# A tower of embedding, attention and routed experts on one core: VectorE's small operations dealt out among its products, and the order of TensorE's ups around the down

## The reference, cut to what matters

```python
z = jnp.einsum('nd,sdr->nsr', layernorm(h), P)
scores = jnp.einsum('nsr,smr->nsm', z, C)
topv, topi = jax.lax.top_k(scores, K)
w = jax.nn.softmax(topv, axis=-1)
hid = jax.nn.gelu(jnp.einsum('nsr,nskrh->nskh', z, W1[sidx, topi]) + b1[sidx, topi])
yl = jnp.einsum('nskh,nskhr->nskr', hid, W2[sidx, topi]) + b2[sidx, topi]
comb = jnp.einsum('nskr,nsk->nsr', yl, w).reshape(N, S * R)
out = h + jax.nn.gelu(comb @ G1 + g1b) @ G2 + g2b
```

## Time and profile before

| what | value |
| --- | --- |
| median of 3 runs | 2905.35 us |
| lowest and highest | 2901.58 and 2911.56 us |
| profiled execution, its own time | 2918.95 us |
| its span | 2917.2 us |
| TensorE matmul busy | 2477.4 us (85%) |
| VectorE busy | 1895.8 us (65%) |
| ScalarE busy | 1200.4 us (41%) |
| GpSimd busy | 1155.5 us (40%) |
| mean granted TensorE clock | 0.926 |

### The profile page before, as it was taken

How to read it: one execution, slowest core, us unless ns; L and a number is a source line. 1 busy time by engine, 2 the same in 40 slices (tenths; PEclk the granted TensorE clock), 3 DMA queues, 4 the chain that set the end, 5 groups by cost and what they waited for, 6 DMA issues and landing times. The chain is left out here.

```text
span 2917.2 us, 42124 instructions
## 1 busy us (share of the span) xinstructions
PE 2477.4 (85%) x16000; PEld 1240.8 (43%) x16000; DVE 1895.8 (65%) x3858; ACT 1200.4 (41%) x1617; POOL 1155.5 (40%) x781
## 2 busy tenths in 40 slices
PE   3556999999999999999999996048888888888898
PEld 1223555565555556555555653022323323232232
DVE  5865565565655656565555654147878888788786
ACT  3421333333333333333333332035656666566565
POOL 5000475666757566575756654021120111201010
PEclk9788999999999999999999998558989999798899
DMA  1002000000010000000000002810101011010100
GB/s 45 11 22 55 7 1 9 1 9 9 1 30 1 9 1 9 9 1 9 1 2 1 3 1 10 72 36 1 24 1 24 1 24 24 1 24 1 24 6 6
DMA packets 78699, 38.51 MB, mean 13 GB/s; under 512 B 62937, under 2 KB 71193, under 8 KB 77849
## 3 DMA queue, kind: packets, MB, share of 16 engines
q1 hardware_dynamic: 76320, 30.98, 6.2%
q10 hardware_dynamic: 640, 1.69, 0.5%
q0 software_dynamic: 1536, 3.15, 0.4%
HBM read 21.93 MB, written 10.49 MB: 11 GB/s over the span
## 5 line engine op out<-in xcount | busy, mean ns | idle before, releaser
L588 POOL TENSOR_TENSOR acc<-acc,pT 128x1024 f32<-128x1024 f32 (+3 forms) x412 | 830.0, 2015 | 243.7 <-ACT pT L907 210.4
L1615 DVE TENSOR_TENSOR hw<-hid,banks 128x512 f32<-128x512 f32 x1024 | 645.7, 683 | 192.0 <-PE banks L1358 187.3
L907 ACT ACTIVATE pT<-banks 128x1024 f32<-128x1024 f32 x480 | 405.7, 896 | 831.1 <-PE banks L661 818.2
L787 DVE TENSOR_REDUCE part<-banks 128x2 f32<-128x1024 f32 (+3 forms) x432 | 438.3, 1044 | 311.7 <-PE banks L637 310.0
L1487 ACT ACTIVATE hid<-banks 128x1024 f32<-128x1024 f32 x512 | 499.5, 1022 | 333.3 <-PE banks L1348 314.7
L1348 PE MATMUL banks<-zst,w1c 50*128 50x512 f32 x1024 | 425.9, 582 | 29.2 <-ACT hid L1487 23.3
L1358 PE MATMUL banks<-wT,select 64*128 64x512 f16 x1024 | 357.5, 421 | 61.6 <-DVE hw L1615 56.9
L677 PE MATMUL banks<-pT,v 128*64 128x512 f32 (+3 forms) x1920 | 404.7, 542 | 1.5 <-POOL pT L576 1.5
L1366 PE MATMUL banks<-hw,w 128*32 128x512 f32 x2048 | 302.0, 664 | 1.4 <-DVE hw L1615 0.8
L1358 PEld LDWEIGHTS banks<-wT,select 64*128 64x128 f16 x1024 | 98.9, 98 | 439.9 <-DVE hw L1615 355.7
L637 PE MATMUL banks<-kh,qh 64*128 64x512 f32 (+1 forms) x960 | 191.1, 393 | 14.5 <-ACT pT L907 5.6
(11 more groups left out here) (183 smaller groups left out, 2901.0 us busy)
## 6 DMA issues: line engine op xcount, KB each, us to landing
zst<-z_scratch SPq DMA_DIRECT2D x48, 128.0 KB, 4.4
z_scratch<-zp SPq DMA_DIRECT2D x8, 512.0 KB, 3.5
out_h<-o SPq DMA_DIRECT2D x8, 384.0 KB, 2.7
xT_scratch<-xs_hi SPq DMA_DIRECT2D x4, 512.0 KB, 2.7
xt_hi<-xT_scratch SPq DMA_DIRECT2D x2, 1024.0 KB, 5.6
w1c<-raw1p ACTq DMA_DIRECT2D x12, 132.0 KB, 4.6
w1c<-raw1p SPq DMA_DIRECT2D x12, 132.0 KB, 4.1
wo<-in_L_attn_W_O SPq DMA_DIRECT2D x12, 96.0 KB, 1.9
```

The source lines that it names most:

```text
L588: pool.tensor_tensor(acc[:, G % 2, :, off:CH], acc[:, G % 2, :, off:CH], pT[:, slot, :, 0:w], ALU.add).then_inc(summed, 1)
L787: last = dve.tensor_reduce(to[:, :, c:c + 1], both[:, :, 0:whole], AX.X, ALU.max)
L907: act.activation(pT[:, J % PSLOTS, :, 0:CH - off], both[:, :, 0:CH - off], ACT.Exp, scale=E ** -0.5)\
L1615: dve.tensor_tensor(hw[:, n % 2, q, :], hid[:, n % 2, q, :], ring_bank(("w", g, n, q)), ALU.mult).then_inc(mixed, 1)
```

## The change

The diff, without the lines of whole functions that only change their arguments (mix now makes one block and not two; normalise and the main loops go through pairs (n, q) and not steps n):

```diff
-        Z_AT = {16: (0,), 17: (1,), 20: (2,)}
-        PREP_AT = {12: (3, 4), 14: (5, 6), 26: (7,), 27: (8,), 28: (9,), 29: (10,)}
+        Z_AT = {11: (0,), 12: (1,), 13: (2,)}
+        PREP_AT = {5: (3, 4), 7: (5, 6), 24: (7,), 25: (8,), 27: (9,), 28: (10,)}
         OUT_AT = {1: (0,), 2: (1,), 3: (2,)}
-        EXP_AT = 18
-        SPLIT_AT = 22
-        BIAS_AT = (18, 21)
+        EXP_AT = 17
+        BIAS_AT = (18, 22)
+        BEST_FROM, MARK_FROM = 8, 16
+        KEEP_AT = {(20, 2): 0, (21, 2): 1, (24, 0): 2, (24, 2): 3}
+        HIGH_AT = {(23, 1): 0, (26, 1): 1}
+        DEN_AT, RECIPROCALS_AT = (16, 0), (20, 0)
+        SUMS_AT, VARIANCE_AT, REFINE_AT, SPLIT_AT = (5, 0), (7, 0), (9, 0), (15, 3)
+        TAKE_OUT_AT = {(3, 1): 0, (4, 1): 1}
...
             def divide(g, part):
-                pool.wait_ge(marked, 2 * g + part + 1)
+                pool.wait_ge(marked, 4 * g + 2 * part + 2)
...
-            def up(g, n, pair, which):
+            def up(g, n, pair, which, beside=None):
                 if which == 0:
                     need(pe, gelu_done, g * (2 * NSTEP) + 2 * n - 1 + pair)
-                low_rows = work(n)[2 * pair][1] < NJ // 2
-                i = 2 * pair + (which + 1 if low_rows else which) % 2
+                    first_of[pair] = 2 * pair
+                    if beside is not None:
+                        gw, nw, iw = beside
+                        first_of[pair] += work(nw)[iw][1] < NJ // 2
+                i = first_of[pair] if which == 0 else 4 * pair + 1 - first_of[pair]
...
                     spread_weights(g, n, 2)
                     if next1[0] < NG:
-                        up(*next1, 1, 0)
+                        up(*next1, 0, 1)
                     if g or n:
                         down(*last1)
                     spread_weights(g, n, 3)
                     if next1[0] < NG:
-                        up(*next1, 1, 1)
+                        up(*next1, 1, 0, (g, n, 3))
                         if next1[1] == 0:
                             pe.wait_ge(w_copied, next1[0] * 4 + 4)
                         spread_weights(*next1, 0)
-                    if next2[0] < NG:
-                        up(*next2, 0, 0)
-                    if next1[0] < NG:
+                        up(*next1, 1, 1)
                         spread_weights(*next1, 1)
                     if next2[0] < NG:
-                        up(*next2, 0, 1)
+                        up(*next2, 0, 0, (*next1, 1))
...
-            def top_four(g, k):
+            def best(g, m):
+                k, r = divmod(m, GT * S // 4)
                 t2, half = divmod(k, 2)
-                dve.wait_ge(side_free, freed_at["prep", g, 3 + k])
-                dve.memset(holder[:, k:k + 1], 0.0)
-                for t in (2 * t2, 2 * t2 + 1):
-                    for q in range(NQ):
-                        i = (half * NQ + q) * GT + t
-                        last = dve.max(top[:, i, :], sc[:, i, :])
-                if k == 3:
+                if r == 0:
+                    dve.wait_ge(side_free, freed_at["prep", g, 3 + k])
+                    dve.memset(holder[:, k:k + 1], 0.0)
+                i = (half * NQ + r % NQ) * GT + 2 * t2 + r // NQ
+                last = dve.max(top[:, i, :], sc[:, i, :])
+                if m == GT * S - 1:
                     link(last)
...
-            def mark(g, part):
-                for i in range(part * GT * S // 4, (part + 1) * GT * S // 4):
-                    last = dve.match_replace(scr[:, i, :], top[:, i, :], sc[:, i, :], TAKEN)
-                if part == 3:
+            def mark(g, i):
+                last = dve.match_replace(scr[:, i, :], top[:, i, :], sc[:, i, :], TAKEN)
+                if i % (GT * S // 4) == GT * S // 4 - 1:
                     link(last)
...
             def keep_marked(g, part):
-                half = slice(part * GT * S // 2, (part + 1) * GT * S // 2)
-                dve.scalar_tensor_tensor(ew[:, half, :], scr[:, half, 0:M], TAKEN, ew[:, half, :],
+                quarter = slice(part * GT * S // 4, (part + 1) * GT * S // 4)
+                dve.scalar_tensor_tensor(ew[:, quarter, :], scr[:, quarter, 0:M], TAKEN, ew[:, quarter, :],
                                          ALU.is_equal, ALU.mult).then_inc(marked, 1)
...
+            def choose(g, n, q):
+                if BEST_FROM <= n < BEST_FROM + 8:
+                    best(g, (n - BEST_FROM) * NQ + q)
+                if (n, q) == DEN_AT:
+                    denominators(g)
+                if MARK_FROM <= n < MARK_FROM + 8:
+                    mark(g, (n - MARK_FROM) * NQ + q)
+                if (n, q) == RECIPROCALS_AT:
+                    reciprocals(g)
+                if (n, q) in KEEP_AT:
+                    keep_marked(g, KEEP_AT[n, q])
+                if (n, q) in HIGH_AT:
+                    high_weights(g, HIGH_AT[n, q])
...
             for g in range(NG):
-                for n in range(NSTEP):
-                    mix(g, n, (0, 1))
-                    if g and n in (3, 4):
-                        take_out(g - 1, n - 3)
+                for n, q in GAPS:
+                    mix(g, n, q)
+                    if g and (n, q) in TAKE_OUT_AT:
+                        take_out(g - 1, TAKE_OUT_AT[n, q])
                     if g < NG - 2:
-                        normalise(g + 2, n)
-                    mix(g, n, (2, 3))
+                        normalise(g + 2, n, q)
                     if g < NG - 1:
-                        prepare(g + 1, n)
-                    if n == SPLIT_AT and g < NG - 2:
-                        split_z(g + 2)
+                        choose(g + 1, n, q)
```

More of the change, by code:

```diff
@@ L1410, in _ @@
             pe.wait_ge(w_copied, 4)
+            first_of = [0, 0]
             for n, pair in ((0, 0), (0, 1), (1, 0)):
                 up(0, n, pair, 0)
-                up(0, n, pair, 1)
+                if (n, pair) != (1, 0):
+                    up(0, n, pair, 1)
             for i in (0, 1):
@@ L1607, in high_weights, with mix @@
                 dve.tensor_copy(wsp[:, half, :, 0, :], by_half).then_inc(w_cast, 1)
-            def mix(g, n, blocks):
-                if (g or n > 1) and 0 in blocks:
+            def mix(g, n, q):
+                if (g or n > 1) and q == 0:
                     dve.wait_ge(down_done, g * NSTEP + n - 1)
-                for q in blocks:
-                    dve.wait_ge(gelu_done, g * (2 * NSTEP) + 2 * n + q // 2 + 1)
-                    dve.wait_ge(spread, g * (NQ * NSTEP) + NQ * n + q + 1)
-                    dve.tensor_tensor(hw[:, n % 2, q, :], hid[:, n % 2, q, :], ring_bank(("w", g, n, q)),
-                                      ALU.mult).then_inc(mixed, 1)
+                dve.wait_ge(gelu_done, g * (2 * NSTEP) + 2 * n + q // 2 + 1)
+                dve.wait_ge(spread, g * (NQ * NSTEP) + NQ * n + q + 1)
+                dve.tensor_tensor(hw[:, n % 2, q, :], hid[:, n % 2, q, :], ring_bank(("w", g, n, q)),
+                                  ALU.mult).then_inc(mixed, 1)
             def take_out(g, k):
@@ L1624, in take_out @@
                                   g2b_bc[:, :].unsqueeze(1).to_broadcast([P, 2, D]), ALU.add).then_inc(out_taken, 1)
-            def prepare(g, n):
-                if 14 <= n < 18:
-                    top_four(g, n - 14)
-                if n == 17:
+            def choose(g, n, q):
+                if BEST_FROM <= n < BEST_FROM + 8:
+                    best(g, (n - BEST_FROM) * NQ + q)
+                if (n, q) == DEN_AT:
                     denominators(g)
-                if 18 <= n < 22:
-                    mark(g, n - 18)
-                if n == 22:
+                if MARK_FROM <= n < MARK_FROM + 8:
+                    mark(g, (n - MARK_FROM) * NQ + q)
+                if (n, q) == RECIPROCALS_AT:
@@ L1634, in prepare, with normalise @@
                     reciprocals(g)
-                if n in (22, 23):
-                    keep_marked(g, n - 22)
-                if n in (24, 25):
-                    high_weights(g, n - 24)
-            def normalise(g, n):
-                if n == 7:
+                if (n, q) in KEEP_AT:
+                    keep_marked(g, KEEP_AT[n, q])
+                if (n, q) in HIGH_AT:
+                    high_weights(g, HIGH_AT[n, q])
+            def normalise(g, n, q):
+                if (n, q) == SUMS_AT:
@@ L1643, in normalise @@
                     sums(g)
-                if n == 13:
+                if (n, q) == VARIANCE_AT:
                     variance(g)
-                if n == 15:
+                if (n, q) == REFINE_AT:
                     refine(g)
+                if (n, q) == SPLIT_AT:
+                    split_z(g)
+            GAPS = [(n, q) for n in range(NSTEP) for q in range(NQ)]
             for g in range(2):
-                for n in range(NSTEP):
-                    normalise(g, n)
-                split_z(g)
@@ L1653, in _ @@
-            for n in range(NSTEP):
-                prepare(0, n)
+                for n, q in GAPS:
```

(11 more changed lines are left out.)

## The result

The changed kernel takes 2965.23 us (median of 4 runs, 2962.24 to 2966.89) against 2906.17 us for the kernel before: ratio 1.0201, 95% interval 1.0182 to 1.0221. It is 59 us slower. The forecast was 2941 us with a range of 2885 to 2985, and slower at 0.72. The profiled execution took 2965.44 us, span 2963.7 us, where the sum made against the profiled execution of before gave 2955.

A forecast was written before the change was run, and what follows sets the result against it. A chain through gelu, up and down set the 3.1 us step; after the change TensorE binds at 2.70 us. Steps, side work and waits sum to 986 us against 950.6, so 2955 profiled and 2941 us forecast, range 2885 to 2985.

The forecast's parts named there:

- The order of the ups: Experts' stage: no up waiting for the newest gelu precedes the down; clean step 3.1 to 2.70 us, 86.4 us a group.
- the circle that the prediction priced second: Clean step by way of VectorE: last product, hand-over, spreading and up, down, spreading to the next product, 2.68 us.
- Singly dealt: VectorE's largest findings and marks between products cost 0.14 and 0.20 us each; what exceeds 2.70 adds 7.9 us a group.
- The scores' wait: Scores moved from step 12 to 5: TensorE waits 9.0 us for z rows in groups 1 to 6; bounds 6 and 12.
- The weights' wait: Weights turned from step 24, not 26: TensorE waits 3.5 us for GpSimd's low half in seven groups; bounds 2 and 5.
- Banks held longer: Spreadings wait for ScalarE's later side copies; per group 0.5 us after mixture, 2.0 scores, 1.9 x and z, 3.6 weights.
- The sum: Experts' stage: groups of 118, five of 130.5, 125 and 90.3 us, together 986 us against 950.6, 36 us more.
- From the profiled execution to the median: Whole kernel: profiled execution to come to 2955 us, less 13.6 us it stood above the median, giving 2941 us.
- Half clock: Rival: granted clock falls to 1.2 GHz behind a gap, 3.4 us in each of seven groups; 2965 us, chance 0.18.
- The surpluses meet: Rival: VectorE's surplus in steps 16 to 24 is paid during TensorE's waits, 76 us less; 2865 us, chance 0.17.
- No change: Rival: half of the overlap of VectorE's surplus with TensorE's waits, 38 us; 2903 us, chance 0.08.
- serial pairs: Rival: spreading and up run one after the other, a step takes 3.5 us; over 3050 us, chance 0.07.

The follow-up runs named there:

- e7: The kernel before with the new order of the ups alone, tables and VectorE's batches of eight kept: 2899.40 us, 0.9964 of the kernel before.
- e4: Changed kernel with z bounce ahead of the output, GpSimd's first low half ahead of the second divide, ScalarE's copies ahead of the gelu: 2852.48 us, 0.9808 of the kernel before.
- e8: The kernel before with VectorE's largest findings and marks alone dealt out, two behind each product in the same steps: 2891.10 us, 0.9924 of the kernel before.
- e1: Changed kernel with SyncE's loop alone altered, z rows of group g + 2 bounced ahead of the output of group g: 2914.13 us, 1.0013 of the kernel before.
- e3: Changed kernel with ScalarE's copies of side items ahead of the first gelu of the step after next: 2945.04 us, 1.0127 of the kernel before.
- e5: Changed kernel with 38 float16 matmuls on 64 rows put on TensorE ahead of the z wait: 2995.37 us, 1.0292 of the kernel before.
- e10: Changed kernel with 38 matmuls on all 128 rows put on TensorE ahead of the z wait: 2961.15 us, 1.0173 of the kernel before.
- e2: Changed kernel with GpSimd's first low half of the weights ahead of the second divide: 2932.51 us, 1.0081 of the kernel before.

## Why the prediction was right or wrong

**The order of the ups.** Right in size: 2.66 us a clean step (2.70 forecast), last group 90.1 us (90.3). The bound is another than the text says. It has TensorE full, 4 x 0.43 + 1.0, but the three pairs behind the down take 0.96 us together and TensorE stands 0.28 us in the step for VectorE. What sets it is the circle that the prediction priced second, at 2.68: last product, spreading and up, down, spreading, next product. The two prices lay so near each other that the number doesn't tell them apart; the rows do. Side work adds to the step all the same: in e7 steps without it gain 0.4 us and those with it nothing, and in e4 a turned weight adds 0.6 us (3.3 against 2.7). Why the 0.28 us don't cover part of that was not tested. The sign that the gelus would no longer come in back-to-back pairs didn't show.

**Singly dealt.** Right in the price, 0.73 us for a product with its largest finding. The 7.9 us of this term can't be added up from the items as the text lists them, which come to about 11; some 7.9 is left if steps 11 to 13, 17, 18, 22 and 24 aren't counted, where another item is longer, and the text doesn't say so. Step 10, which has largest findings and nothing else, took the 2.9 us of the text. That a batch cost more than its own time was in the sum only as what the new steps took; e8 shows 20 us for it alone.

**The scores' wait.** Right in place, cause and size: 9.0 us forecast, 52.5/6 = 8.75 measured, and e1 takes it away by SyncE's order alone, which shows that the output ahead of the bounce was the cause. The row of before, 11.75 us from the output's issue to the last landing, held (11.6); the prediction's estimate of some 4.5 us for two small transfers, from the fixed 2.0 us in the Trainium skill (DMA: Bandwidth & Descriptors, section Anatomy of one DMA), did not describe this chain, which is a store of 512 KB and six loads of 128 KB and took 11.1 us from the store's issue at 2620.56 to the scores. The measurement decides.

**The weights' wait.** Right in place and cause; mis-sized: 3.5 us forecast, the wait is 25.5 us in six groups from 2080 us on, 4.25 each, and taking it away gave 4.7 in each of seven.

**Banks held longer.** Right in mechanism and wrong in size: the sum had 8.0 us a group, e3 measured 2.9. Each wait of a spreading was smaller (weights 12.8/18 = 0.7 us, z 3.7/5 = 0.7, mixture 2.2/7 = 0.3, against 0.9, 0.9 and 0.5); of four turned weights three were waited for in each of six groups and not four; the scores' waits came to 3.0/6 = 0.5 us a group against 2.0, and steps 6 and 8 didn't move when e3 took them away; and the step after a held one ran at 2.5 us, below a clean one. This is the term of the sum that failed most.

**The sum.** 986 us for the stage, 1000.5 measured: 118 to 122.0 in the first group, 130.5 to 132.4 on average in the next five, 125 to 126.4 in the seventh, 90.3 to 90.1 in the last. The miss of 14.5 us is small in part by luck: the holds, 5 us a group too many, stood against what the sum had too small: 1.2 a group at the weights, and steps 6 and 8. Two small prices are also not what their rows give: a turned weight stands at 0.6 us without the 0.2 taken off, and the mixture up at 0.85 where 9.4/8 - 0.2 is 0.97. Steps 6 and 8 hold the scores; with the holds gone e4 still took 5.5 and 4.8 us in them. The granted clock is part of that. A stretch in the z wait of the changed kernel, one right behind it and a later one (length, busy PE, PEld, DVE, ACT, POOL, granted clock, DMA share, GB/s):

```profile
2625.40:2632.20 6.80, 0.55 (x6) 0.58 (x6) 0.00 (x0) 0.00 (x0) 0.00 (x0) 0.50 0.70 104
2632.20:2639.10 6.90, 6.90 (x40) 3.14 (x38) 2.80 (x4) 3.78 (x5) 0.00 (x0) 0.51 0.00 1
2649.30:2656.10 6.80, 6.26 (x42) 2.15 (x38) 6.80 (x22) 4.12 (x5) 0.84 (x1) 1.00 0.01 2
```

In e4, without holds, the clock is 1.3 to 1.8 us of step 6 and up to 1.1 us of step 8. How clock and bank waits share these steps in the changed kernel itself wasn't told apart.

**From the profiled execution to the median.** The forecast took off 13.6 us because the profiled execution of before lay above its median. The profiled execution of the changed kernel lay at its own median (2965.44 against 2965.23). Against profiled executions the miss is 2965 against 2955; the other 14 us are this step. In the later series the kernel before ran at a median of 2911 us, so part of it is the spread of the kernel before. That spread goes with the clock: of its 17 runs beside e5 to e8 the shortest, 2899.40 us, had a mean granted clock of 0.935, and the longest, 2920.33 us, one of 0.926.

**The rivals.** *Half clock*: its time, 2965, is the measured one, but its reason carries only part of the difference. The clock did fall, in step 6 in all six groups with the z wait and in step 25 in all seven (granted 0.6 to 0.8 on average there), but for part of that time TensorE stood and waited: behind the z wait it cost some 1 to 3 us a group by e4 and e10, e2 leaves some 3 us in all for it behind the weights' wait, and in e1 it fell in step 6 without any wait. *The surpluses meet*: against it stand the steps with dealt operations right behind the z wait, which take VectorE's full price (2.9 us in step 10), and that e1, e2 and e3 gained as much together as one by one. *No change* and *serial pairs* are excluded by the rows.

## What to carry to other kernels

Moving a step earlier moves it against every queue that feeds it: here the scores passed SyncE's output and the bounce behind it, and some 30 us of better schedule (e7 and e8) went under 52 us of wait at the scores and 30 at the weights (4.25 us in each of seven groups), which one exchange in SyncE's loop and one in GpSimd's gave back. When a stage is bound by a circle of waits, work beside it is free; once the circle is cut, each item beside the work shows with its price again (0.6 us for a turned weight here, which is all of its busy time) and has to be put where another engine is behind. When two circles are priced within 1% of each other, read in the rows which one holds, before building on the name of the bound. Price a wait for a buffer with the steps after it, since they catch up part of it.

## What the runs showed of the hardware that was not expected

TensorE's granted clock stood at 0.50 for over 13 us in e5 while it made float16 matmuls on 64 rows with no gap, and in two of six equal places it stood at 1.00; with 128 rows (e10) it was at 1.00 through five of six. So a TensorE that makes one matmul after the other isn't always one that keeps 2.4 GHz. A spreading on one half of the rows and an up on the other take 0.43 us together (2410.86 to 2411.29 in the earlier trace rows), and so does the up alone (2854.72 to 2855.15 in the earlier trace rows). Several such pairs in a row take less than 0.43 us each: three took 0.96 us in the changed kernel (2905.22 to 2906.18). A largest finding or a mark put between two products of 128x512 costs VectorE the same 0.13 and 0.20 us as in a row of eight (with a mark between them products start 0.80 us apart, as at 2676.69 and 2677.49 in the changed kernel).
